# Stage B's second norm and its router by batch: batch 0's among batch 1's attention, batch 1's among batch 0's experts

## The reference, cut to what matters

```python
xn = _rmsnorm(x, gamma1)
... # q, k, v, rotary positions, causal attention with 16 heads of 64
attn_out = ctx @ o_w + o_b + xn
an = _rmsnorm(attn_out, gamma2)
shared = gelu(an @ sh_w1 + sh_b1) @ sh_w2 + sh_b2
logits = an @ router_w + router_b              # 31 experts
aff = softmax(logits)
topv, topi = top_k(aff, 3)
gates = sum(one_hot(topi, 31) * topv[..., None], axis=-2)
h = gelu(einsum('bsd,edh->besh', an, re_w1) + re_b1)
routed = einsum('bse,besh,ehd->bsd', gates, h, re_w2) + einsum('bse,ed->bsd', gates, re_b2)
return shared + routed + an + attn_out
```

## Time and profile before

| | us |
|---|---|
| Median of 3 runs | 2681.18 |
| The runs | 2678.3, 2681.18, 2685.4 |
| The profiled execution | 2693.05 |
| Its span | 2691.2 |
| TensorE, VectorE, ScalarE busy | 2259.9, 1687.6, 1132.4 |
| Last projection of stage B's attention ends | 907.07 |
| Stage C's first matmul | 938.49 |
| First expert's first matmul | 942.17 |

### The profile page before, as it was taken

One profiled execution on the slowest core, in us unless ns is written; L12 is line 12 of the kernel. 1 busy time (PEld: TensorE's weight loads), 2 busy tenths in 40 slices (PEclk: granted clock), 3 DMA queues, 4 the chain that ended last, 5 costly groups with the idle time before them and its releaser, 6 DMA issues.

```text
span 2691.2 us, 32165 instructions
## 1 busy us (share of the span) xinstructions
PE 2259.9 (84%) x11288; PEld 897.5 (33%) x11288; DVE 1687.6 (63%) x3866; ACT 1132.4 (42%) x1855; POOL 142.9 (5%) x143
## 2 busy tenths in 40 slices
PE   5999969789999598887788688788878869877898
PEld 2333334343333275223222232322322233232433
DVE  4666648546565567775675577568467657745464
ACT  1333323102222133465466366456636636653321
POOL 0000000011111030000000000000000000010000
PEclk8999979859999699799798799889979989988999
DMA  3000000030000011000010010001001000020000
GB/s 141 1 1 0 1 0 1 3 107 1 1 1 1 12 41 42 5 21 2 24 41 1 24 41 2 24 1 42 1 24 41 2 24 4 22 99 0 1 0 8
DMA packets 38033, 54.34 MB, mean 20 GB/s; under 512 B 5073, under 2 KB 34546, under 8 KB 36338
## 3 DMA queue, kind: packets, MB, share of 16 engines
q1 hardware_dynamic: 37874, 52.28, 6.2%
HBM read 32.34 MB, written 0.52 MB: 12 GB/s over the span
## 4 chain that ended last, share of the span: by engine, by line
PE 38%; DVE 10%; ACT 7%; issue 4%; SPq 0%; DMA 0%; ACTq 0%; DVEq 0%
PE ps L1762 7%; PE ps L1744 5%; ACT big L2220 4%; PE ps L1725 4%; DVE C_nm L2392 4%; PE ps L1807 2%; PE ps L1886 2%; PE ps L1993 2%; PE ps L1898 2%; PE ps L1989 2%; PE ps L2014 2%; PE ps L1905 2%; PE ps L1863 2%; ACT big L2300 2%; PE ps L1914 2%
## 5 line engine op out<-in xcount | busy, mean ns | idle before, releaser
L2392 DVE TENSOR_REDUCE C_nm<-ps 128x1 f32<-128x512 f32 x768 | 501.1, 685 | 184.2 <-PE ps L1725 180.4
L2220 ACT ACTIVATE big<-ps 128x512 f32<-128x512 f32 x768 | 427.8, 596 | 235.6 <-PE ps L1744 226.3
L1725 PE MATMUL ps<-C_attn 62*128 62x512 bf16 x768 | 277.6, 418 | 57.9 <-DVE C_nm L2392 47.0
L1744 PE MATMUL ps<-C_attn 64*128 64x512 bf16 x768 | 253.4, 398 | 62.3 <-ACT big L2220 51.7
L1762 PE MATMUL ps<-big,C_attn 128*32 128x512 f32 x1536 | 213.8, 630 | 13.3 <-ACT big L2220 13.3
L1725 PEld LDWEIGHTS ps<-C_attn 62*128 62x128 bf16 x768 | 63.6, 94 | 304.6 <-DVE C_nm L2392 158.8
L713 DVE TENSOR_REDUCE A_nm<-ps 128x2 f32<-128x1024 f32 x64 | 77.5, 1212 | 117.2 <-PE ps L500 117.1
L1744 PEld LDWEIGHTS ps<-C_attn 64*128 64x128 bf16 x768 | 59.2, 93 | 274.5 <-ACT big L2220 203.1
L2300 ACT ACTIVATE big<-ps,C_biasx 77x512 f32<-77x512 f32 x192 | 115.5, 678 | 55.9 <-PE ps L1890 55.8
L2486 DVE TENSOR_REDUCE C_nmx<-ps 128x4 f32<-128x308 f32 x192 | 78.5, 471 | 61.4 <-PE ps L1867 61.2
L650 ACT ACTIVATE A_p<-ps 128x1024 f32<-128x1024 f32 x64 | 65.6, 1025 | 112.6 <-PE ps L528 112.6
(11 more groups left out here) (379 smaller groups left out, 3817.6 us busy)
## 6 DMA issues: line engine op xcount, KB each, us to landing
C_attn<-C_first SPq DMA_DIRECT2D x144, 128.0 KB, 2.4
C_w<-in_C_w SPq DMA_DIRECT2D x6, 1090.0 KB, 5.1
C_attn<-in_D_ew SPq DMA_DIRECT2D x4, 1536.0 KB, 10.2
big<-in_B_ew SPq DMA_DIRECT2D x8, 514.0 KB
normw_later<-in_norm_w SPq DMA_DIRECT2D x1, 2304.0 KB, 15.8
A_w<-in_A_w SPq DMA_DIRECT2D x2, 1024.0 KB, 9.2
A_w<-in_A_w SPq DMA_DIRECT2D x2, 768.0 KB, 5.6
B_w<-in_B_w SPq DMA_DIRECT2D x1, 1536.0 KB, 11.1
```

What stands on the lines that cost most here:

```text
L1725: pe.matmul(ps[:, bank, :], lhsT=qs[side(hp, MAX_ROW), b, 2 * q + pq, t * P:(t + 1) * P], rhs=ks[side(hp, MAX_ROW), b, 2 * q + pq, :], sta ...
L1744: pe.matmul(ps[:, bank, :], lhsT=ks[side(1 - hp, HALF), b, 2 * q + pq, kt * P:(kt + 1) * P], rhs=qs[side(1 - hp, HALF), b, 2 * q + pq, :], ...
L2220: act.activation(prob[:, kt % 2, pq, 1 - hp, :], ps[:, bank, :], ACT.Exp, scale=SCALE)\
L2392: dve.tensor_reduce(nm[:, q % 2, t, pq, hp:hp + 1], ps[:, bank, :], AX.X, ALU.max, negate=True).then_inc(emptied[bank], 1)
```

## The change

The second norm and the router of stage B are cut by batch into steps of a class `Router`, and these steps are laid elsewhere.

Batch 0's are given to `self_attention_block` as a `tail` whose functions are called at the end of each (u, kt) on each engine: batch 0's output is transposed and added at (10, 0), the statistics stand at (11, 0), the four parts of the root at (11, 1) to (12, 0), the normalising at (12, 1), its transposes and their copy at (14, 3), the logits at (15, 0), the softmax from (15, 1), the gates at the very end. Batch 1's output is only copied out at the end of the block. Blocks "B2n" and "B3" are gone, and the router's two transfers are issued with the other loads at the head of stage B.

Batch 1's steps get places in `first_plan` among batch 0's experts: its output is transposed and added first, then come the norm, the router and the gates, and its residual and bias behind them. The ten "consts" steps move back by three experts.

```diff
@@ self_attention_block, TensorE @@
                 if p == 0 and b:
-                    pe.wait_ge(oT_ready, b)
+                    pe.wait_ge(oT_ready if tail is None else y_added, b)
...
+                    if tail is not None:
+                        if (u, kt) == (PAIRS + 2, 0):
+                            turn_out(0, OUT_BANK)
+                        if (u, kt) == (N - 2, TB - 1):
+                            pe.wait_ge(max_done, N * TB)
+                        tail.tensor(pe, u, kt, S_BANK)
...
@@ self_attention_block, VectorE @@
+                    if tail is not None:
+                        if (u, kt) == (PAIRS + 2, 0):
+                            add_out(0, OUT_BANK)
+                            dve.wait_ge(y_added, 1)
+                        tail.vector(dve, u, kt, S_BANK)
                 if u:
                     normalise(u - 1)
             add_up(N - 1, 3)
+            if tail is not None:
+                tail.vector(dve, N, 0, S_BANK)
             invert(N - 1, 0)
             invert(N - 1, 1)
             normalise(N - 1)
@@ stage_b @@
-        self_attention_block(nc, m, "B1", wa, wa_loaded, rope=(m.cos, m.sin), bias=m.bias)
-    norm_block(nc, m, "B2n", rms_row=R_G2)
-    router_b(nc, a, m, e.gates, e.gT, w_loaded)
+        tail = batch0_tail(m, e, Router(m, "B3", e, small, 0), w_loaded)
+        self_attention_block(nc, m, "B1", wa, wa_loaded, rope=(m.cos, m.sin), bias=m.bias, tail=tail)
@@ class Router: steps of four tiles each @@
+    def root(self, dve, part):
+        m, c = self.m, self.c
+        if part == 0:
+            seed_steps(c, dve, m, TB, True)
+        else:
+            y, t, u, v = m.rs[:, 0:TB], m.lnt[:, 0:TB], m.lnu[:, 0:TB], m.lnv[:, 0:TB]
+            c.after(dve.tensor_tensor(t, y, y, ALU.mult))
+            c.after(dve.scalar_tensor_tensor(u, t, -0.5, v, ALU.mult, ALU.mult))
+            c.after(dve.scalar_tensor_tensor(y, u, 1.5, y, ALU.add, ALU.mult))
...
+    def share(self, dve):
+        c, aff = self.c, self.aff[:, :, 0:E_R]
+        dve.wait_ge(self.e_done, 1)
+        c.after(dve.tensor_reduce(self.ssum[:, :, 0], aff, AX.X, ALU.add))
+        c.after(dve.reciprocal(self.ssum, self.ssum))
+        c.after(dve.tensor_tensor(aff, aff, self.ssum.broadcast_to([P, TB, E_R]), ALU.mult))
...
@@ batch0_tail, TensorE @@
+        if (u, kt) == (N - 2, 3):
+            r.turn(pe, m.ps[:, bank, :]).then_inc(r.turned, 1)
+        if (u, kt) == (N - 1, 0):
+            pe.wait_ge(w_loaded, 16 * EXPERT_LOADS)
+            pe.wait_ge(r.hT_ready, 1)
+            r.logits(pe, m.ps[:, bank + 1, :]).then_inc(r.logits_done, 1)
+        if u == N:
+            r.turn_gates(pe, m.ps[:, bank, :]).then_inc(r.g_turned, 1)
@@ batch0_tail, VectorE @@
+        if (u, kt) == (N - 1, 1):
+            dve.wait_ge(w_loaded, 16 * EXPERT_LOADS)
+            dve.wait_ge(r.logits_done, 1)
+            r.shift(dve, m.ps[:, bank + 1, :])
+        if (u, kt) == (N - 1, 3):
+            r.share(dve)
+        if (u, kt) == (N, 0):
+            r.choose(dve)
...
@@ first_plan @@
-    plan["PE"] += [(B_FIRST - 4, "bias_b", b, 0) for b in range(B)]
-    plan["DVE"].append((B_FIRST - 4, "residual", 0, 0))
-    plan["DVE"] += [(B_FIRST + 1, "bias_b", b, 0) for b in range(B)]
+    step = lambda k: B_FIRST + k * B_STRIDE
+    plan["PE"] += [(step(0) - 5, "turn_out_b", 1, 0), (step(0) - 4, "bias_b", 0, 0), (step(7) + 1, "turn_b", 1, 0),
+                   (step(9) + 1, "logits_b", 1, 0), (step(17) + 1, "turn_gates_b", 1, 0), (step(20) + 1, "bias_b", 1, 0)]
+    plan["ACT"] += [(step(7) + 12, "copy_b", 1, 0), (step(11) + 12, "exp_b", 1, 0)]
...
+    plan["DVE"] += [(step(2 + i) + 31, "root_b", 1, i) for i in range(4)]
+    plan["DVE"] += [(step(6) + 11, "apply_b", 1, 0), (step(10) + 11, "shift_b", 1, 0), (step(12) + 31, "share_b", 1, 0),
+                    (step(14) + 31, "choose_b", 1, 0), (step(18) + 11, "take_gates_b", 1, 0),
+                    (step(19) + 11, "residual", 1, 0), (step(21) + 1, "bias_b", 1, 0)]
...
-        plan["DVE"].append((B_FIRST + (18 + i) * B_STRIDE + 31, "consts", 0, i))
+        plan["DVE"].append((B_FIRST + (21 + i) * B_STRIDE + 31, "consts", 0, i))
```

More of the change, by code:

```diff
@@ L565, in project_out, with turn_out @@
                 if p == 0 and b:
-                    pe.wait_ge(oT_ready, b)
+                    pe.wait_ge(oT_ready if tail is None else y_added, b)
                 pe.matmul(ps[:, OUT_BANK, :], lhsT=weight(n, WO), rhs=ctx[:, n % 2, :], start=p == 0,
                           stop=p == PAIRS - 1).then_inc(out_done, 1)
+            def turn_out(b, bank):
+                pe.wait_ge(oT_ready, b + 1)
+                for t in range(TB):
+                    last = pe.transpose(ps[:, bank, t * P:(t + 1) * P], oT[:, b, t * P:(t + 1) * P], m.ident[:])
+                last.then_inc(o_turned, 1)
             pe.wait_ge(w_loaded[0], 16)
@@ L789, in _ @@
             normalise(N - 1)
-            for b in range(B):
-                dve.wait_ge(o_turned, b + 1)
-                y = m.y[:, b * TB:(b + 1) * TB, :]
-                dve.tensor_tensor(y, y, ps[:, S_BANK + b, :].rearrange("p (t d) -> p t d", t=TB), ALU.add)\
-                    .then_inc(y_added, 1)
+            if tail is not None:
+                tail.vector(dve, N, 1, S_BANK)
+            else:
+                for b in range(B):
+                    add_out(b, S_BANK + b)
 def cross_attention_block(nc, m, name, w, w_loaded):
@@ new lines, in batch0_tail, with tensor, scalar, vector @@
+def batch0_tail(m, e, r, w_loaded):
+    N = B * PAIRS
+    tail = Mem()
+    tail.out = e.out
+    def tensor(pe, u, kt, bank):
+        if (u, kt) == (N - 2, 3):
[6 more added lines that the diff above has]
+            r.turn_gates(pe, m.ps[:, bank, :]).then_inc(r.g_turned, 1)
+    def scalar(act, u, kt, bank):
+        if (u, kt) == (N - 2, 3):
+            act.wait_ge(r.turned, 1)
+            r.copy(act, m.ps[:, bank, :]).then_inc(r.hT_ready, 1)
+        if (u, kt) == (N - 1, 1):
+            r.exps(act)
+    def vector(dve, u, kt, bank):
+        if (u, kt) == (PAIRS + 3, 0):
+            r.begin(dve)
+            r.stats(dve)
+        for part in range(4):
+            if (u, kt) == (PAIRS + 3 + (part + 1) // 4, (part + 1) % 4):
+                r.root(dve, part)
+        if (u, kt) == (PAIRS + 4, 1):
+            r.apply(dve)
+        if (u, kt) == (N - 1, 1):
+            dve.wait_ge(w_loaded, 16 * EXPERT_LOADS)
[5 more added lines that the diff above has]
+            r.choose(dve)
+        if (u, kt) == (N, 1):
+            dve.wait_ge(r.g_turned, 1)
+            r.take_gates(dve, m.ps[:, bank, :]).then_inc(r.gT_ready, 1)
+    tail.tensor, tail.scalar, tail.vector = tensor, scalar, vector
+    return tail
@@ L2017, in apart @@
                 def apart(name, b, e):
-                    if name == "bias_b":
+                    if name == "turn_out_b":
+                        bank = fill((name, b))
+                        for t in range(TB):
+                            last = pe.transpose(ps[:, bank, t * P:(t + 1) * P], e_b.out[:, t * P:(t + 1) * P], m.ident[:])
+                        last.then_inc(filled[bank], 1)
+                    elif name == "turn_b":
+                        pe.wait_ge(rt.xn_ready, 1)
+                        bank = fill((name, b))
+                        rt.turn(pe, ps[:, bank, :]).then_inc(filled[bank], 1)
+                    elif name == "logits_b":
+                        drained(pe, ("turn_b", b))
+                        bank = fill((name, b))
+                        rt.logits(pe, ps[:, bank, :]).then_inc(filled[bank], 1)
+                    elif name == "turn_gates_b":
+                        pe.wait_ge(rt.gates_ready, 1)
+                        bank = fill((name, b))
+                        rt.turn_gates(pe, ps[:, bank, :]).then_inc(filled[bank], 1)
+                    elif name == "bias_b":
+                        if b:
+                            drained(pe, ("turn_gates_b", b))
                         bias_b(b)
@@ L2330, in apart @@
                 def apart(name, b, e):
-                    if name == "expert":
+                    if name == "copy_b":
+                        bank = arrived(act, ("turn_b", b))
+                        rt.copy(act, ps[:, bank, :]).then_inc(emptied[bank], 1)
+                    elif name == "exp_b":
+                        rt.exps(act)
+                    elif name == "expert":
                         expert(e)
```

191 lines of the change are left out of this document (123 added, 68 removed).

## The result

The changed kernel takes 2675.96 us (median of 20 runs, 2666.75 to 2688.15), the kernel before 2682.76 (20 runs, 2675.24 to 2697.2). The ratio is 0.9971, 95% interval 0.9958 to 0.9984: by that ratio 7.8 us faster (4.3 to 11.3; the medians differ by 6.8), where 20.9 were forecast.

A forecast was written before the change was run, and what follows sets the result against it. Between batch 1's attention and the experts a serial chain left TensorE, the bound engine, standing. 28.1 + 0.9 - 0.45 - 2.8 - 3.6 - 1.3 = 20.9 us; 2681.2 - 20.9 = 2660.3 us, 8 in 10 within 2651 to 2670.

The forecast's parts named there:

- Start of stage C: End of batch 1's attention: stage C starts at 910.4 us instead of 938.45, 28.1 us earlier.
- 0.45 in the attention: Batch 0's norm and router work inside batch 1's attention: 0.45 us lost, between nothing and 1.2.
- delay by the shares: Batch 0's sum, reciprocal and product on VectorE ahead of pair 14's context delay attention's end by 0.85 us (0.55 to 1.1).
- First expert: Stage C's start to its first expert: four transposes and eight bias records take 2.85 us, 0.9 us won.
- The wait at the transposes: Among batch 0's experts: TensorE waits 2.4 us for VectorE ahead of batch 1's normed-row transposes; 1.45 at best, 2.9 at worst.
- rival C: Something in stage C, a load or GpSimd's constants, doesn't move with its start; gain under 8 us, 2673 to 2683; 5%.
- Exponential: Among batch 0's experts: two table loads around batch 1's exponential on ScalarE make TensorE wait 1.0 us (0 to 1.8).
- Choice of gates: Among batch 0's experts: VectorE's block of 2.1 to 2.3 us makes TensorE wait 0.2 us (0 to 1.1).
- TensorE's own records: Among batch 0's experts: batch 1's transposes, logits, gate transposes and bias on TensorE, 2.8 us lost.
- the prediction's own sign of being wrong: Batch 0's experts, 32 steps of 1.75 us, stretched by over 10 us instead of 6.4 and the clock's 2.2.
- Clock (-1.3): TensorE's clock: 2.2 us lost after the wait at the transposes, 0.9 won in attention's last pairs; 1.3 us lost in all.
- Carrying over 11.9 us to the median: The profiled execution lay 11.9 us above the runs' median, unexplained by the stretches' rows; the difference was carried over unchanged.

The follow-up runs named there:

- second profile of before: The kernel before, unchanged, profiled once more as a single execution: span 2682.7 us, 8.5 under its first profile.
- the selects away: Changed kernel with GpSimd's clearing of C_selx and its eight selects moved behind its part of the first unit's K: 0.9913, 2661.41 us.
- memsets: Changed kernel with each of GpSimd's eight selects replaced by a memset of the same tile; a single execution, read by its profile alone.

## Why the prediction was wrong

- **Start of stage C (28.1, less 0.45 in the attention).** Right. 0.8 us of delay by the shares (0.85), the choice hidden, the block ended by the copy of the gates, 1.0 us to the next stage (912.17, so not later than 913). By the first profile of before it is 30.9 us, by the second 26.6; the difference is the clock's.
- **First expert (+0.9)**: 26.98 us at the expert against 26.32 at the start, 0.7. Right.
- **The wait at the transposes (2.4, at worst 2.9): 7.16.** This is the step that failed. It took VectorE's durations from the block before, "0.2 each, whose width hardly matters", and 1.1 for the normalising; there GpSimd stood idle. With the selects away the wait is 1.68, and the time 0.9913, 23 us under before: the forecast's 20.9 lies inside that interval (18 to 29), in part by luck, since only 8.9 of the 15.6 us between the two kernels are accounted for. The prediction had even looked at GpSimd: rival C held that its constants are issued at the stage's own start, and took that as a reason for calm. It was what brought them onto the norm. The measured 2675.96 lies in rival C's band, but by the opposite mechanism: nothing of stage C stayed behind, all of it moved. The Trainium skill ("SBUF — State Buffer", Who interferes with whom) has the rule that speaks against this change, and I weighed others.
- **Exponential (1.0): 0.89. Choice of gates (0.2): none. TensorE's own records (2.8)**: 14.6 us are lost from the first expert to the end of the experts, less waits (0.34 + 0.82 + 7.16 + 0.89) and 1.8 of half clock, 3.6, so 0.8 more than forecast. In all, the experts were stretched by 14.6 us where 8.6 were forecast; over 10 was the prediction's own sign of being wrong.
- **Clock (-1.3).** Behind the transposes 1.8 us were lost, close to the forecast 2.2, but behind a wait three times as long. Whether 2.4 us of waiting would have brought the clock down stays open: among the experts, behind 1.68 us (selects moved) and 2.06 (memsets) it stayed up, behind 4.59 and more it fell. In the last pairs of attention the clock was at full from 891 to 905 us and gave 2.9 us against before's first profile, not 0.9 (the last output matmul came 2.5 us later in place of 4.6 + 0.8); but before's second profile does that without the change.
- **Carrying over 11.9 us to the median.** The prediction said that no row explains the excess of the profiled execution. The second profile of before is 8.5 us shorter, and 4.0 of these lie in the very stretch that the change takes apart, so an execution like that one had that much less to win.
- **Not in the sum at all**: the two loads at the head of stage B, 1 to 3 us.

Put together: to the first expert 29.4 us were forecast (28.1 + 0.9 - 0.45 + 0.9), and 31.6 came against the first profile of before, 27.3 against the second. Among the experts 8.6 were to be lost (2.8 + 3.6 + 2.2), and 14.6 were (14.1 against the second); the waits of 0.34, 0.82 and 7.16 us in place of 2.4 make 5.9 of the difference. The loads' head of stage B took 2.7 in this profile. That leaves 14.3 us by the first profile of before and 10.5 by the second, where 7.8 and 8.3 were measured, the first of them between 4.3 and 11.3. So the failed wait is worth some 6 us of the 13 that are missing; most of the others are the loads and a profile of before that was not typical, by single profiles and no better than 2 us each. What stays open is how the clock's phases in the attention of stage C come about, by which two profiles of before drift up to 8 us apart there; the spread of the runs is of that size.

## What to carry to other kernels

When a stage starts earlier, everything that hangs on its start moves too, also the work of an idle engine at 5%: list what now runs beside what, engine by engine, and price moved operations by rows in which the same neighbours are active. A chain of small VectorE operations with two inputs in SBUF should not share a stretch with GpSimd's selects, and TENSOR_SCALAR not even with its memsets; sums with one input in PSUM may. And profile the kernel before twice: a gain read off a stretch that happened to run at half clock is not all there to be won.

## What was not expected of the hardware

- VectorE is held until the GpSimd instruction ends, whatever its own size: an operation on four columns took 1.28 us, to 929.51, where a select ended too. For each of the selects, which wait for one another, two operations get through: one in the gap (928.04, 0.16 us) and one held to the select's end (928.24, 1.28). Between two memsets without a gap none gets through (6.91 us).
- The same waits of 2.94 and 2.21 us left TensorE at half clock in one execution of a program and at full clock in another.
